# First-layer attention: inverse row sums by a trip through memory instead of TensorE transposes, with head staging moved ahead of GpSimd's products

## The chip, the cores and the metric

One core of a Trainium2 chip runs the whole program. The metric is the device time of one execution in microseconds (us). Engines: TensorE (PE, with its weight loads shown as PEld), VectorE (DVE), ScalarE (ACT), GpSimd (POOL) and SyncE (SP), which here only issues DMAs.

## What is computed

Two layers in float32 on an input of 8 x 32 x 32 x 512. The change touches the first one alone. Per image (1024 tokens, 512 channels, 8 heads of 64):

```python
x_norm = _group_norm(x, gn_scale, gn_bias).reshape(b, seq, c)
qkv = x_norm @ w_qkv + b_qkv                       # q, k, v as 8 heads of 64
weight = jnp.einsum('bhld,bhsd->bhls', q * scale, k * scale)
weight = jax.nn.softmax(weight, axis=-1)
out = jnp.einsum('bhls,bhsd->bhld', weight, v)
out = out.transpose(0, 2, 1, 3).reshape(b, seq, c)
out = out @ w_out + b_out
return (x_flat + out).reshape(b, h, w, c)
```

The second layer (a deformable attention with its own projections, a depthwise convolution and an MLP) takes the first one's output from memory, and is the same before and after.

## The kernel before

The first layer is written by hand in Bass: five instruction streams, one for each engine, with semaphores between them. Each stream loops over the 8 images; inside an image the order of the instructions is the order of the code, and there is no scheduler. Precision is kept by splitting each float32 operand of a product into a high part and a remainder (`kh`/`kl`, `ph`/`pl`, `wqkv_hi`/`wqkv_lo`), so one product is made of two or three matmuls.

**Units and pairs.** A unit u is one head and one tile of 128 queries; an image has U = 64 units, 8 a head. A pair b is two units, 32 pairs in an image, four a head. Every engine runs a loop over a step i_, and does in step i_:

- TensorE (`tensor_image`, L409): half of the products with v of pair (i_ - 5) // 2 (`output`, 8 matmuls at L484), the scores of unit i_ (`scores`, four matmuls at L448 and L449 into two PSUM banks), then the eight transposes of the exponents of unit i_ - 2 (`transposes`, L463), in two groups of four, each into one of two banks. In the odd steps, where `part == 0`, `output` also transposes the broadcast inverse row sums of the two units (L479) into the upper half of the bank in which the products of the pair are summed.
- VectorE (`vector_image`, loop at L623): the negated maximum of the scores (L626), in even steps the fold sum of a pair (L634), the two subtractions that make the low part `pl` of unit i_ - 2 (L643), and in odd steps the reciprocals of a pair's row sums (L647).
- ScalarE (`scalar_image`, loop at L563): in even steps two copies out of PSUM for a pair, `fold_t` (L570) and `fold_r` (L574), then the high part `ph` of unit i_ - 2 (L584, twice) and the exponent of unit i_ with its row sum (L591).
- GpSimd (`gpsimd_image`): for each pair the product of the fold sum with `fold_r` (L725), written over the head's q in `qk`; in between, the parts of `stage` (L704 to L716), which makes high and low parts of the next head's q and k.
- SyncE (`sync_image`): copies of each head's q and k into `qs` and `kl` (L390, L391), two tile sets in turn, then loads for the next image (L396) and of the residual (L403), and stores of the result (L406).

The high and low part of v stand side by side, so a pair's products come out as 128 partitions, of which two halves must be added: `fold_t` moves one half across, and the fold sum adds it to the other. Even heads use partitions 0 to 63 for this, odd heads 64 to 127 (`own_half`). Each 64 x 256 sum is then scaled by 1/row sum per query, and since the queries lie along the free dimension there, the inverse must stand along it too. That is what the transposes at L479 and the copy `fold_r` make.

**Waits that matter here.** The first transposes group of a unit waits for the subtraction of the same group one unit before (`pl_ok`), since there are two banks. The scores of unit i_ wait for the exponent of unit i_ - 2 and, at the first tile of a head, for the whole staging of the head (`staged`). Fold sums and `fold_r` have two buffers, so fold sum b waits for product b - 2 (`att_ok`). When four pairs of an even and four of an odd head are done, a quarter of the attention's result is split into high and low parts, in two halves behind steps 16c + 23 and 16c + 25 (`SPLIT_AT`, ScalarE L599 and VectorE L651); the last quarter is split in four pieces behind steps 64 to 70.

**The tail of an image.** Behind step 63 only the rest of the pairs is left; TensorE fills the time with transposes of the next image's tokens (`turn`, L190) and with the output projection (L510), and ScalarE copies those transposes out (`keep_tile`, L194) behind the last piece of the split.

## Time and profile before

| what | value |
| --- | --- |
| median of 3 runs (lowest to highest) | 4038.05 us (4036.7 to 4046.57) |
| the profiled execution: its time, its span | 4036.7 us, 4035.0 us |
| mean granted share of TensorE's clock | 0.987 |
| busy: TensorE, its weight loads, VectorE | 3865.6, 3260.5, 2966.9 us |
| busy: ScalarE, GpSimd | 2507.4, 1638.9 us |
| first weight load of scores, last of the L479 transposes | 92.5 us, 2294.2 us |

Busy time is the union of an engine's instructions. Matmuls are pipelined and their ends are modelled, so two neighbours overlap in the rows, and the distance between starts tells what one costs; the weight loads give these starts best. In a timeline row the first number is the start, the second the time from the first start to the last end of the merged instructions, xN their number, and the bracket the idle time before and what ended it.

### The profile page before, as it was taken

The numbers are of one execution on the slowest core, as the hardware profiler recorded it, in microseconds if no ns is written. First come the engines' busy times: TensorE is split into PE (matmuls) and PEld (weight loads), VectorE is DVE, ScalarE is ACT, GpSimd is POOL, SyncE is SP. The second block draws the span as 40 slices with busy tenths as digits, with TensorE's granted clock in tenths as the row PEclk, the third lists the DMA queues.
The fourth block names the chain that finished last, engine by engine and source line by source line (L and its number), as shares of the span: only waits on it lengthen the run. The fifth ranks groups of instructions, "written<-read, shape, count | busy, mean of one in ns | idle before, by whom it ended". The sixth has DMA issues, their size and how long they took to land. (4 is left out here: it accounts for less than half of the span.)

```text
span 4035.0 us, 63980 instructions
## 1 busy us (share of the span) xinstructions
PE 3865.6 (96%) x22126; PEld 3260.5 (81%) x22126; DVE 2966.9 (74%) x5158; ACT 2507.4 (62%) x5497; POOL 1638.9 (41%) x1935
## 2 busy tenths in 40 slices
PE   8999999999999999999999988999999999999999
PEld 6888888888888888878878856777777777777777
DVE  3984984975966957938849737878787878787876
ACT  3883864865846847838838615656565656565656
POOL 1332432422432432323324305555555555555554
PEclk9999999999999999999999989999999999999999
DMA  2221221221221221222212132222222222222221
GB/s 86 43 64 45 50 64 42 44 79 36 64 63 27 59 63 32 54 63 43 64 42 50 55 110 61 79 70 77 71 78 70 79 70 78 70 77 70 77 74 58
DMA packets 117736, 252.28 MB, mean 63 GB/s; under 512 B 17772, under 2 KB 34216, under 8 KB 117416
## 3 DMA queue, kind: packets, MB, share of 16 engines
q1 hardware_dynamic: 112808, 231.41, 21.3%
q0 software_dynamic: 4608, 16.78, 1.3%
q8 instruction: 180, 2.95, 0.3%
q14 instruction: 140, 1.15, 0.1%
HBM read 97.12 MB, written 33.55 MB: 32 GB/s over the span
## 5 line engine op out<-in xcount | busy, mean ns | idle before, releaser
L626 DVE TENSOR_REDUCE a_neg_max<-a_ps 128x1 f32<-128x1024 f32 x512 | 625.0, 1222 | 336.7 <-PE a_ps L449 336.7
L725 POOL TENSOR_TENSOR a_qk<-a_fold_s,a_fold_r 64x256 f32<-64x256 f32 x256 | 191.4, 748 | 1228.8 <-DVE a_fold_s L634 1228.8
L584 ACT ACTIVATE a_ph<-a_ps 128x512 fp32r<-128x512 f32 x1024 | 556.9, 593 | 171.3 <-PE a_ps L463 168.3
L643 DVE TENSOR_TENSOR a_pl<-a_ps,a_ph 128x512 fp32r<-128x512 f32 x1024 | 654.7, 680 | 8.9 <-ACT a_ph L584 5.7
L591 ACT ACTIVATE a_prob<-a_ps,a_neg_max 128x1024 f32<-128x1024 f32 x512 | 572.3, 1118 | 17.6 <-DVE a_neg_max L626 11.8
L463 PEld LDWEIGHTS a_ps<-a_ident,a_prob 128*128 128x128 f32 x4096 | 469.8, 140 | 112.6 <-issue 46.8
L463 PE MATMUL a_ps<-a_ident,a_prob 128*128 128x128 f32 x4096 | 540.7, 274 | 17.3 <-DVE a_pl L643 16.2
L484 PE MATMUL a_ps<-a_ph,a_v 128*128 128x256 f32 x2048 | 550.7, 302 | 0.0
L484 PE MATMUL a_ps<-a_pl,a_v 128*128 128x256 f32 x2048 | 509.2, 282 | 0.0
L448 PE MATMUL a_ps<-a_kh,a_qs 128*128 128x512 f32 x1024 | 408.3, 399 | 12.0 <-POOL a_kl L716 12.0
L449 PE MATMUL a_ps<-a_kl,a_qs 128*128 128x512 f32 x1024 | 404.8, 395 | 0.0
L1853 POOL TENSOR_SCALAR b_prob<-b_prob,b_row_inv 128x256 f32<-128x256 f32 x512 | 247.5, 483 | 365.1 <-DVE b_row_inv L1734 329.3
L484 PEld LDWEIGHTS a_ps<-a_pl,a_v 128*128 128x128 f32 x2048 | 389.3, 190 | 0.3
L484 PEld LDWEIGHTS a_ps<-a_ph,a_v 128*128 128x128 f32 x2048 | 386.5, 189 | 0.3
L1628 DVE SCALAR_TENSOR_TENSOR b_ps<-b_qpad,b_dww,b_ps 128x256 f32<-128x256 f32 x704 | 294.2, 483 | 4.8
L1550 ACT ACTIVATE b_prob<-b_ps,b_neg_max 128x256 f32<-128x256 f32 x512 | 236.5, 483 | 40.5 <-DVE b_neg_max L1739 39.9
L1298 PE MATMUL b_ps<-b_qpad,b_diag 128*128 128x256 f32 x928 | 232.4, 409 | 0.0
L448 PEld LDWEIGHTS a_ps<-a_kh,a_qs 128*128 128x128 f32 x1024 | 193.7, 189 | 43.9 <-POOL a_kl L716 21.7
L1298 PEld LDWEIGHTS b_ps<-b_qpad,b_diag 128*128 128x128 f32 x928 | 176.4, 190 | 51.0
L449 PEld LDWEIGHTS a_ps<-a_kl,a_qs 128*128 128x128 f32 x1024 | 194.1, 190 | 25.0
L250 PE MATMUL a_ps<-a_xh,wqkv_hi 128*128 128x512 f32 x512 | 200.0, 391 | 4.1 <-DVE wqkv_lo L355 4.1
L250 PE MATMUL a_ps<-a_xh,wqkv_lo 128*128 128x512 f32 x512 | 199.9, 390 | 0.0
(265 smaller groups left out, 9316.0 us busy)
## 6 DMA issues: line engine op xcount, KB each, us to landing
a_qs<-a_qk SPq DMA_DIRECT2D x128, 256.0 KB, 3.7
a_kl<-a_qk SPq DMA_DIRECT2D x128, 256.0 KB, 4.4
a_xtok<-in_x SPq DMA_DIRECT2D x64, 256.0 KB, 4.6
b_xs<-x SPq DMA_DIRECT2D x64, 256.0 KB, 4.6
b_qs<-b_qh SPq DMA_DIRECT2D x64, 256.0 KB, 3.3
b_qs<-b_ql SPq DMA_DIRECT2D x64, 256.0 KB, 3.8
b_z<-x SPq DMA_DIRECT2D x64, 256.0 KB, 3.7
out<-b_ot SPq DMA_DIRECT2D x64, 256.0 KB, 2.0
```

Source lines behind the costliest of these rows:

```text
L250: mm = pe.matmul(ps[:, g % 8, :], a, b, start=k == 0 and e == 0, stop=k == CT - 1 and e == 2)
L448: pe.matmul(bank, q_, kh[:, j, n], start=True, stop=False)
L449: mm = pe.matmul(bank, q_, kl[:, j, n], start=False, stop=True)
L463: mm = pe.transpose(ps[:, 4 + n % 2, kk * P:(kk + 1) * P], prob[:, u % 2, kt * P:(kt + 1) * P], ident[:])
L484: mm = pe.matmul(ps[:, 6 + b % 2, 0:256], v[:, h, kt, :], q_[:, b % 2, kt, :], start=kt == 0 and e == 0, stop=kt == TT - 1 and e == 1)
L584: act.activation(ph[:, b % 2, 4 * g:4 * g + 4, (u % 2) * P:(u % 2 + 1) * P], ps[:, 4 + n % 2, :].rearrange("p (k q) -> p k q", k=4), ACT.C ...
L591: act.activation(prob[:, i_ % 2, :], ps[:, 2 * (i_ % 2):2 * (i_ % 2) + 2, :] .rearrange("p a b -> p (a b)"), ACT.Exp, bias=neg_max[:, i_:i ...
L626: dve.tensor_reduce(neg_max[:, i_:i_ + 1], ps[:, 2 * (i_ % 2):2 * (i_ % 2) + 2, :] .rearrange("p a b -> p (a b)"), AX, ALU.max, negate=Tru ...
L643: dve.tensor_tensor(pl[here], ps[:, 4 + n % 2, :].rearrange("p (k q) -> p k q", k=4), raw(ph[here]), ALU.subtract).then_inc(pl_ok, 1)
L1298: mm = pe.matmul(ps[:, c, 0:NS], diag[:, e % DIAGS, :], window(c, n), start=first, stop=last)
L1628: dve.scalar_tensor_tensor(dst, window(c, n), dww[:, c, n:n + 1], grid(partial), ALU.mult, ALU.add).then_inc(tap, 1)
L1853: pool.tensor_scalar(prob[:, u % 2, t, :], prob[:, u % 2, t, :], row_inv[:, c:c + 1], 0.0, ALU.mult, ALU.add).then_inc(sc_ok, 1)
```

## The change

Inverse sums take another way. After the reciprocals of pair b, SyncE writes the 128 x 2 values of `row_inv` to a row of a small tensor in memory (`inverses_out`) and, once that write has landed, reads the row back as a broadcast over 64 partitions into `fold_r` (`inverses_in`), one pair behind. The L479 transposes and the `fold_r` copy are gone. The row in memory is ordered (query, unit of the pair), so GpSimd's product reads `fold_r` with a stride of two. `fold_r` and `fold_s` have four buffers instead of two. The reciprocals move from the odd step to the end of the even step before it. GpSimd does each part of `stage` ahead of the product beside which it stood. SyncE's stream is rearranged around the pairs: head copies, the write of pair b, the read of pair b - 1, and in the last eight pairs one load each for the next image. Waits on `fold_cp` count one copy a pair instead of two.

```diff
--- before.py
+++ after.py
@@ -84,6 +84,9 @@
     NB = TOK // 256
     U = NH * TT
     QSCALE = 1.0 / HD
+    ROWS = 4
+
+    inv_row = nc.dram_tensor("a_inv_row", [U // 2, 256], F32, kind="Internal").ap()
 
     with ExitStack() as ctx:
         def sem(name):
@@ -107,8 +110,8 @@
         row_sum = R.take("a_row_sum", [P, U])
         row_inv = R.take("a_row_inv", [P, U])
         fold_t = R.take("a_fold_t", [P, 256])
-        fold_r = R.take("a_fold_r", [P, 2, 256])
-        fold_s = R.take("a_fold_s", [P, 2, 256])
+        fold_r = R.take("a_fold_r", [P, ROWS, 256])
+        fold_s = R.take("a_fold_s", [P, ROWS, 256])
         qk = R.take("a_qk", [P, 2 * CT, TOK])
         v_at = R.at
         v = R.take("a_v", [P, NH, TT, P], F32R)
...
@@ -380,7 +386,8 @@
             at = counted(r)
             more = r + 1 < n_images
 
-            for h in range(NH):
+            def copies(h):
+
                 p, j = h // 2, h % 2
                 sp.wait_ge(qk_sb, at(qk_sb, 4 if p == 0 else 4 + 4 * p))
                 if h >= 2:
@@ -389,11 +396,36 @@
                     rows_ = slice(HD * half, HD * half + HD)
                     sp.dma_start(raw(qs[rows_, j, :]), qk[own_half(h), p, :]).then_inc(s_ld[j], 16)
                     sp.dma_start(raw(kl[rows_, j, :]), qk[own_half(h), CT + p, :]).then_inc(s_ld[j], 16)
-            if more:
-                for j in range(2):
-                    sp.wait_ge(s_ld[j], at(s_ld[j], 64 * (NH // 2)))
-                for t in range(TT):
+
+            def inverses_out(b):
+
+                sp.wait_ge(inv_ok, at(inv_ok, b + 1))
+                sp.dma_start(inv_row[b].rearrange("(p n) -> p n", n=2), row_inv[:, 2 * b:2 * b + 2])\
+                  .then_inc(iv_st[b % 2], 16)
+
+            def inverses_in(b):
+
+                sp.wait_ge(iv_st[b % 2], at(iv_st[b % 2], 16 * (b // 2 + 1)))
+                if b >= ROWS:
+                    sp.wait_ge(att_ok, at(att_ok, b - ROWS + 1))
+                sp.dma_start(fold_r[own_half(b // NB), b % ROWS, :], inv_row[b].partition_broadcast(HD))\
+                  .then_inc(iv_ld[b % ROWS], 16)
+
+            copies(0)
+            copies(1)
+            for b in range(U // 2):
+                if (b + 1) % NB == 0 and (b + 1) // NB + 1 < NH:
+                    copies((b + 1) // NB + 1)
+                inverses_out(b)
+                if b >= 1:
+                    inverses_in(b - 1)
+                if more and b >= U // 2 - TT:
+                    t = b - (U // 2 - TT)
+                    if t == 0:
+                        for j in range(2):
+                            sp.wait_ge(s_ld[j], at(s_ld[j], 64 * (NH // 2)))
                     sp.dma_start(xtok[:, t, :], x[r + 1, t * P:(t + 1) * P, :]).then_inc(x_ld[t], 16)
+            inverses_in(U // 2 - 1)
             sp.wait_ge(score, at(score, U))
             for t in range(TT):
                 if t == 2:
@@ -468,16 +500,10 @@
 
                 h = b // NB
                 if part == 0:
-                    pe.wait_ge(inv_ok, at(inv_ok, b + 1))
                     if b == 0:
                         pe.wait_ge(vl_ok, at(vl_ok, n_v))
                     if b >= 2:
                         pe.wait_ge(fold_add, at(fold_add, b - 1))
-                        pe.wait_ge(fold_cp, at(fold_cp, 2 * b - 2))
-                    for n in range(2):
-                        u = 2 * b + n
-                        pe.transpose(ps[:, 6 + b % 2, 256 + n * P:256 + (n + 1) * P],
-                                     row_inv[:, u:u + 1].to_broadcast([P, P]), ident[:])
                 pe.wait_ge(pl_ok, at(pl_ok, 4 * b + 3 + part))
                 for kt in range(4 * part, 4 * part + 4):
                     for e, q_ in enumerate((ph, pl)):
@@ -494,7 +520,6 @@
                     pe.wait_ge(pl_ok, at(pl_ok, 2 * U))
                 elif t in (2, 3):
                     pe.wait_ge(fold_add, at(fold_add, U // 2 + t - 3))
-                    pe.wait_ge(fold_cp, at(fold_cp, U + 2 * (t - 3)))
                 else:
                     pe.wait_ge(out_ok, at(out_ok, t - 3))
                 n = slice(t * P, (t + 1) * P)
@@ -568,10 +593,6 @@
                     if b >= 1:
                         act.wait_ge(fold_add, at(fold_add, b))
                     act.activation(fold_t[own_half(h), :], ps[other_half(h), 6 + b % 2, 0:256], ACT.Copy)\
-                        .then_inc(fold_cp, 1)
-                    if b >= 2:
-                        act.wait_ge(att_ok, at(att_ok, b - 1))
-                    act.activation(fold_r[own_half(h), b % 2, :], ps[own_half(h), 6 + b % 2, 256:512], ACT.Copy)\
                         .then_inc(fold_cp, 1)
                 if 2 <= i_ < U + 2:
                     u = i_ - 2
@@ -628,10 +649,10 @@
                 if 6 <= i_ <= U + 4 and i_ % 2 == 0:
                     b = (i_ - 6) // 2
                     h = b // NB
-                    dve.wait_ge(fold_cp, at(fold_cp, 2 * b + 2))
-                    if b >= 2:
-                        dve.wait_ge(att_ok, at(att_ok, b - 1))
-                    dve.tensor_tensor(fold_s[own_half(h), b % 2, :], ps[own_half(h), 6 + b % 2, 0:256],
+                    dve.wait_ge(fold_cp, at(fold_cp, b + 1))
+                    if b >= ROWS:
+                        dve.wait_ge(att_ok, at(att_ok, b - ROWS + 1))
+                    dve.tensor_tensor(fold_s[own_half(h), b % ROWS, :], ps[own_half(h), 6 + b % 2, 0:256],
                                       fold_t[own_half(h), :], ALU.add).then_inc(fold_add, 1)
                 if 2 <= i_ < U + 2:
                     u = i_ - 2
@@ -642,9 +663,9 @@
                         dve.wait_ge(ph_ok, at(ph_ok, n + 1))
                         dve.tensor_tensor(pl[here], ps[:, 4 + n % 2, :].rearrange("p (k q) -> p k q", k=4),
                                           raw(ph[here]), ALU.subtract).then_inc(pl_ok, 1)
-                    if u % 2 == 1:
-                        dve.wait_ge(exp_ok, at(exp_ok, u + 1))
-                        dve.reciprocal(row_inv[:, u - 1:u + 1], row_sum[:, u - 1:u + 1]).then_inc(inv_ok, 1)
+                if i_ >= 2 and i_ % 2 == 0 and i_ <= U:
+                    dve.wait_ge(exp_ok, at(exp_ok, i_))
+                    dve.reciprocal(row_inv[:, i_ - 2:i_], row_sum[:, i_ - 2:i_]).then_inc(inv_ok, 1)
                 if i_ in SPLIT_AT:
                     c, n = SPLIT_AT[i_]
                     dve.wait_ge(ah_ok, at(ah_ok, list(SPLIT_AT).index(i_) + 1))
@@ -720,15 +741,17 @@
             stage(1, (0, 1, 2))
             for b in range(U // 2):
                 h = b // NB
-                pool.wait_ge(fold_add, at(fold_add, b + 1))
-                pool.wait_ge(fold_cp, at(fold_cp, 2 * b + 2))
-                pool.tensor_tensor(qk[own_half(h), h // 2, (b % NB) * 256:(b % NB + 1) * 256],
-                                   fold_s[own_half(h), b % 2, :], fold_r[own_half(h), b % 2, :],
-                                   ALU.mult).then_inc(att_ok, 1)
-                pool.wait_ge(att_ok, at(att_ok, b + 1))
                 k, part = (b + 2) // NB, (b + 2) % NB
                 if 1 <= k <= NH - 2 and part < 3:
                     stage(k + 1, (part,))
+                pool.wait_ge(fold_add, at(fold_add, b + 1))
+                pool.wait_ge(iv_ld[b % ROWS], at(iv_ld[b % ROWS], 16 * (b // ROWS + 1)))
+                pool.tensor_tensor(qk[own_half(h), h // 2, (b % NB) * 256:(b % NB + 1) * 256]
+                                   .rearrange("p (n q) -> p n q", n=2),
+                                   fold_s[own_half(h), b % ROWS, :].rearrange("p (n q) -> p n q", n=2),
+                                   fold_r[own_half(h), b % ROWS, :].rearrange("p (q n) -> p n q", n=2),
+                                   ALU.mult).then_inc(att_ok, 1)
+                pool.wait_ge(att_ok, at(att_ok, b + 1))
             for t in range(TT):
                 pool.wait_ge(r_ld[t], at(r_ld[t], 16))
                 pool.tensor_tensor(tok[t], tok[t], bout[:], ALU.add).then_inc(res_ok, 1)
```

## Rows read from the trace of the kernel before

**Rows 1.** The page's busy time of each engine (us, share of the span, instructions).

```profile
PE 3865.6 (96%) x22126; PEld 3260.5 (81%) x22126; DVE 2966.9 (74%) x5158; ACT 2507.4 (62%) x5497; POOL 1638.9 (41%) x1935
```

**Rows 2.** Groups by line, L479 on TensorE: busy us, mean ns | idle before.

```profile
L479 PE MATMUL a_ps<-a_ident,a_row_inv 128*128 128x128 f32 x512 | 97.8, 273 | 0.6 <-DVE a_row_inv L647 0.6
```

**Rows 3.** Timeline of the weight loads, steps 10 to 12 (even head).

```profile
121.75 0.19 PEld L448 LDWEIGHTS a_ps<-a_kh,a_qs 128*128 128x128 f32 x1
...
123.57 0.25 PEld L479 LDWEIGHTS a_ps<-a_ident,a_row_inv 128*128 128x128 f32 x2
...
124.73 0.19 PEld L448 LDWEIGHTS a_ps<-a_kh,a_qs 128*128 128x128 f32 x1
...
127.48 0.19 PEld L448 LDWEIGHTS a_ps<-a_kh,a_qs 128*128 128x128 f32 x1
```

**Rows 4.** Timeline of VectorE behind the splits of steps 23 and 25.

```profile
164.08 0.69 DVE L651 TENSOR_TENSOR a_a<-a_qk,a_a 128x512 fp32r<-128x512 f32 x1 [0.68 <-ACT a_a L599]
164.69 1.22 DVE L626 TENSOR_REDUCE a_neg_max<-a_ps 128x1 f32<-128x1024 f32 x1
...
172.50 1.27 DVE L643 TENSOR_TENSOR a_pl<-a_ps,a_ph 128x512 fp32r<-128x512 f32 x2
```

**Rows 5.** Weight loads, first of steps 15, 16, 18, 23, 24, 28.

```profile
136.18 0.19 PEld L448 LDWEIGHTS a_ps<-a_kh,a_qs 128*128 128x128 f32 x1
...
139.53 0.19 PEld L448 LDWEIGHTS a_ps<-a_kh,a_qs 128*128 128x128 f32 x1 [0.52 <-POOL a_kl L716]
...
145.24 0.19 PEld L448 LDWEIGHTS a_ps<-a_kh,a_qs 128*128 128x128 f32 x1
...
159.67 0.19 PEld L448 LDWEIGHTS a_ps<-a_kh,a_qs 128*128 128x128 f32 x1
...
162.88 0.19 PEld L448 LDWEIGHTS a_ps<-a_kh,a_qs 128*128 128x128 f32 x1 [0.38 <-POOL a_kl L716]
...
175.16 0.19 PEld L448 LDWEIGHTS a_ps<-a_kh,a_qs 128*128 128x128 f32 x1
```

**Rows 6.** Timeline of VectorE in step 10 (even head).

```profile
123.00 1.23 DVE L626 TENSOR_REDUCE a_neg_max<-a_ps 128x1 f32<-128x1024 f32 x1 [0.26 <-PE a_ps L449]
124.14 0.41 DVE L634 TENSOR_TENSOR a_fold_s<-a_ps,a_fold_t 64x256 f32<-64x256 f32 x1
124.47 1.27 DVE L643 TENSOR_TENSOR a_pl<-a_ps,a_ph 128x512 fp32r<-128x512 f32 x2
```

**Rows 7.** Timeline of VectorE and ScalarE in step 16 (fold of an odd head).

```profile
140.76 1.23 DVE L626 TENSOR_REDUCE a_neg_max<-a_ps 128x1 f32<-128x1024 f32 x1 [0.84 <-PE a_ps L449]
141.19 1.09 ACT L584 ACTIVATE a_ph<-a_ps 128x512 fp32r<-128x512 f32 x2 [0.35 <-PE a_ps L463]
142.01 0.43 DVE L634 TENSOR_TENSOR a_fold_s<-a_ps,a_fold_t 64x256 f32<-64x256 f32 x1
142.47 1.29 DVE L643 TENSOR_TENSOR a_pl<-a_ps,a_ph 128x512 fp32r<-128x512 f32 x2
```

**Rows 8.** Timeline of GpSimd ahead of head 2's first scores.

```profile
136.28 0.74 POOL L725 TENSOR_TENSOR a_qk<-a_fold_s,a_fold_r 64x256 f32<-64x256 f32 x1 [2.87 <-DVE a_fold_s L634]
137.09 2.38 POOL L716 TENSOR_TENSOR a_kl<-a_kl,a_kh 128x1024 fp32r<-128x1024 f32 x1
```

**Rows 9.** Timeline in the tail of the second image: ScalarE, weight loads, TensorE.

```profile
569.85 0.38 ACT L574 ACTIVATE a_fold_r<-a_ps 64x256 f32<-64x256 f32 x1
...
571.69 0.95 PEld L463 LDWEIGHTS a_ps<-a_ident,a_prob 128*128 128x128 f32 x8 [0.79 <-issue]
...
584.00 2.10 PE L190 MATMUL a_ps<-a_ident,a_xtok 128*128 128x128 f32 x16 [0.80 <-ACT a_xt L194]
```

**Rows 10.** Issue of a head copy (timeline of SyncE), and landings by kind (us).

```profile
139.26 1.19 SPq L391 DMA_DIRECT2D a_kl<-a_qk  x1
...
a_kl<-a_qk SPq DMA_DIRECT2D x128, 256.0 KB, 4.4
...
b_kh<-b_kc_hi SPq DMA_DIRECT2D x128, 64.0 KB, 2.1
```

More of the change, by code:

```diff
@@ L163, in layer0 @@
         av_ps, fold_cp, fold_add, att_ok = sem("av_ps"), sem("fold_cp"), sem("fold_add"), sem("att_ok")
+        iv_st, iv_ld = [sem(f"iv_st{i}") for i in range(2)], [sem(f"iv_ld{i}") for i in range(ROWS)]
         ah_ok, al_ok, out_ps, res_ok, out_ok = sem("ah_ok"), sem("al_ok"), sem("out_ps"), sem("res_ok"), sem("out_ok")
@@ L166, in layer0 @@
                    xn_ok, xh_ok, xl_ok, pr_ps, qk_sb, vh_ok, vl_ok, staged, score, max_ok, exp_ok, tr_ps, ph_ok,
-                   pl_ok, inv_ok, av_ps, fold_cp, fold_add, att_ok, ah_ok, al_ok, out_ps, res_ok, out_ok]
+                   pl_ok, inv_ok, av_ps, fold_cp, fold_add, att_ok, *iv_st, *iv_ld, ah_ok, al_ok, out_ps, res_ok, out_ok]
         nums = [s.num for s in cleared]
@@ L368, in layer0 @@
         EACH.update({s_ld[0].num: 256, s_ld[1].num: 256, o_st.num: 16 * TT, pr_ps.num: len(groups), qk_sb.num: n_qk})
-        EACH.update({s.num: U for s in (score, max_ok, exp_ok, fold_cp)})
+        EACH.update({s.num: U for s in (score, max_ok, exp_ok)})
         EACH.update({s.num: 2 * U for s in (tr_ps, ph_ok, pl_ok)})
-        EACH.update({s.num: U // 2 for s in (inv_ok, av_ps, fold_add, att_ok)})
+        EACH.update({s.num: U // 2 for s in (inv_ok, av_ps, fold_cp, fold_add, att_ok)})
+        EACH.update({s.num: 16 * (U // 4) for s in iv_st})
+        EACH.update({s.num: 16 * (U // 2 // ROWS) for s in iv_ld})
         EACH.update({staged.num: STAGE * NH, ah_ok.num: len(SPLIT_AT), al_ok.num: len(SPLIT_AT)})
```

## Prediction

> **What bounds the kernel.** The table of busy time comes first [rows 1]: TensorE 96%, VectorE 74%, ScalarE 62%, GpSimd 41%, over both layers. The change touches the first layer's attention alone, so the second view is its costliest groups: the two transposes of inverse sums in front of each pair of units run 512 times, 0.273 us each [rows 2]. An average hides what a step costs, so the third view is the timeline of TensorE's weight loads, read from one first load of scores (L448) to the next. I call that distance a step; a step i does scores(i), the transposes of unit i-2 and half of the products with v of an earlier pair.
> In a pair of steps of an even head [rows 3] the step that holds the L479 transposes is 124.73 - 121.75 = 2.98 us long (2.97 as a rule), the other 127.48 - 124.73 = 2.75. The remaining instructions are the same, so the two transposes cost 0.22 us of TensorE's stream, not 2 x 0.273: matmuls overlap. TensorE is back to back there, hence it bounds these pairs.
> VectorE is the next bound, and nearly as close. Transposes wait for the subtractions (L643) of the unit before (two PSUM banks), and these come behind the maximum and the fold sum. The place where this loop bites is seen after a split of a finished quarter: there the subtractions end at 172.50 + 1.27 = 173.77 [rows 4] and the scores two steps on start at 175.16 [rows 5], 1.39 us later (rest of the transposes, eight products, nothing else). Below 1.39 this distance can't go. In the even head it is 127.48 - (124.47 + 1.27) = 1.74 [rows 3, 6]: 0.35 to spare. In an odd head it is 145.24 - (142.47 + 1.29) = 1.48 [rows 7, 5]: 0.09 to spare. The reason stands in the starts: in the even head the fold sum starts at 124.14, 0.09 before the maximum ends, and the subtraction at 124.47, 0.08 before the fold's end [rows 6]; in the odd one both start 0.02 to 0.03 after the end [rows 7], and maximum to last subtraction takes 3.00 us instead of 2.74.
> Why odd heads are slower decides a term. At 140.76 ScalarE is not late: it copies into ph at 141.19 after 0.35 us of idling [rows 7], and the fold still waits for the maximum's end. So the copy that the change removes (fold_r) is not what keeps VectorE apart; the partitions are, since odd heads use partitions 64 to 127. The Trainium skill, "VectorE: DVE Perf Modes", section "Two Vector instructions with no wait between them", gives the rule: an instruction whose operands start in another quadrant of 32 partitions than those before it is held until they have finished. By that rule the odd heads stay as slow as they are, since the fold keeps its partitions; without it one would book 0.22 us for their pairs too, as the first rival does. The trace agrees with the rule.
>
> **The change, part by part** (per image; 8 images).
> 1. Inverse transposes gone from TensorE. 30 of the 32 pairs have them between two steps with scores: 11 in even heads, 12 in odd ones, 6 around the splits (part 2) and one at the tail's start (part 3). Even heads: 11 pairs (step 4 and the four of head 0 make 5, and two of each of heads 2, 4, 6 outside the splits) x (2.97 - 2.75) = 2.42 us; the spare 0.35 covers it, and TensorE stays the bound. Odd heads 1, 3, 5: 12 pairs x (1.48 - 1.39) = 1.08; what is late next is the subtraction.
> 2. Heads staged ahead. The first scores of head 2 start late: 139.53 - 136.18 = 3.35 instead of 2.75, behind GpSimd's L716; head 3's 162.88 - 159.67 = 3.21 [rows 5]. L716 starts at 137.09, behind the product at 136.28, before which GpSimd idled 2.87 us [rows 8]. In the new order its 2.38 us fill that idle time and end 3 us or more before the scores. Gain 0.60 at heads 2, 4, 6. At heads 3, 5, 7 nothing: the split just before (steps 23, 39, 55) holds VectorE: its part of the split waits 0.68 us for ScalarE's and ends at 164.77, and the next maximum starts right there, at 164.69 [rows 4], when its scores are long done; from there to 175.16 all hangs on VectorE and ScalarE, which the change leaves as they are. So the 0.46 there, and the 0.22 of the two split pairs, turn into a wait for subtractions. 3 x 0.60 = 1.80.
> 3. ScalarE's fold_r copy gone: 0.38 us beside other work inside the attention, where ScalarE waits for transposes anyway: nothing. In the tail it counts. The ph copy of unit 62 follows fold_r (569.85) at once, and the last transposes (571.69, 0.79 idle) wait for that unit's subtraction [rows 9]: 0.38, and with the maximum a little earlier 0.45. Then the transposes of the last pair, 0.22. Together 0.67. The last pair's fold_r stands between its products and the x copies for which TensorE waits 0.80 us at 584.00 [rows 9]: 0.38 and the gap behind it, 0.40, in the 7 images with a next one.
> 4. Reciprocals one step earlier: 0.15 us of VectorE behind the subtractions of the even step. The exponents were done a step before, so no new wait; the maximum queued behind starts up to 0.1 later, and has the odd step (no fold) to catch up. Nothing. If that cover were gone it is 0.07 a pair, 30 pairs: 2.1 an image.
> 5. The trip through memory: 256 writes of 8 bytes a partition and 256 broadcast reads, on SyncE's queue between head copies and x loads. No row shows such a write; landings run from 2.1 us (64 KB) to 4.4 (head copies) [rows 10]. The reads' issue follows the next pair's write, whose reciprocal ends about 4.1 us into the step (the subtractions end at 125.74 - 121.75 = 3.99 [rows 3, 6], and 0.15 follows); with issues of 1.2 each, as the head copy's [rows 10], and 2.1 the row lands 4.1 + 2.4 + 2.1 = 8.6 us after that step's start, and the sum it meets is ready one pair (5.6) and 2.8 later (124.14 + 0.41 - 121.75), at 8.4. So it is 0.2 late, with 4.4 it is 2.5: GpSimd's product is late then, but nobody waits, since four sum buffers let it fall three pairs (16 us) behind. In the tail the last reciprocal is at 571.7 (an estimate: behind the subtractions for which the transposes of 571.69 waited, 0.6 for the second of them, less the 0.45 of part 3), the write lands by 575.0 (at 4.4: 577.3), the read by 578.3 (582.9), wanted at 580.9, 0.4 before the sum of today: between 2.6 us spare and 2.0 late (16 us over the images). I take spare, the 64 KB row being nearest in size. The residual loads start up to 8 us later, behind the last read; GpSimd adds the first behind the last product, at 582, and by 2.1 the first lands at 581.6: nothing, or 1 to 2 us an image if late.
> 6. Head copies queue behind one write and one read: 1.2 us later, covered by the 3 us by which staging then ends ahead of need. The x loads are spread and ready before step 64. GpSimd reads fold_r with a stride of 2: 0.74 us [rows 8], at most doubled, and hidden but for the last product (up to 0.7 x 8 = 6 us against; taken as 0).
>
> Sum: 2.42 + 1.08 + 1.80 + 0.67 = 5.97, x 8 = 47.8; 0.40 x 7 = 2.8; together 50.6 us. The profiled execution took 4036.7 us (span 4035.0); 4036.7 - 50.6 = 3986.1. The median of the three runs lies 1.35 above: 3987.5, rounded 3988.
>
> **Rivals.**
> - TensorE the bound everywhere: odd heads shed 0.22 too, 12 x 0.13 x 8 = 12 more, and with splits half relieved (3 x 0.2 x 8) 5 more: 3971. For it: fold_r is out of VectorE's wait. Against: [rows 7]. 12%.
> - VectorE the bound in even heads too (the reciprocal in the even step, ScalarE shifted): 11 x 0.13 x 8 = 11 less, and the tail's 8.2 eaten by a late row: 4007. For: 0.35 of spare shrinks to 0.13. Against: the copies get earlier, not later. 18%.
> - The trip decides: SyncE takes a pair's write and read in turn; if issue and landing block it beyond a pair (5.5 us), the product falls behind, after four pairs the fold waits for att_ok, and the excess stands in every pair: at 7 us, 256 x 1.5 = 384 us more, less the 51: 4371. It decides from 5.5 us of SyncE a pair, and turns the gain at 5.7; from rows it is 2 x 1.2 plus a quarter of four copies, 3.6 at most. The Trainium skill, "DMA: Bandwidth & Descriptors", "Specifications", speaks against the change here: below 512 B a write to memory is read, modified and written. No run here shows that yet. 5%.
> - No change: transposes and staging wait hidden anyway. Against it stands 2.98 beside 2.75 in every pair. 4%.
>
> **Chances.** Forecast 61%. Measurement tells 0.3% (12 us) from nothing. Faster: 61 + 12 + 18 = 91%; same 4%; slower 5%. Range 3968 to 4011: its lower end is the first rival, its upper the second; outside lie the last two.
>
> **What would show it.** L479 and the fold_r copy gone. Even-head pairs 5.50 us, odd ones 5.64, with TensorE waiting for the subtraction before the odd step's transposes; first step of heads 2, 4, 6 at 2.75 to 2.9; heads 3, 5, 7 a longer wait behind the split. GpSimd's product starting by the fold sum, seldom by the DMA. Wrong if odd pairs are 5.50 (first rival), if even pairs are above 5.6 (second), if the fold sum waits for a product or SyncE's queue is full (third).

## The result, and the profile after

The changed kernel takes 4025.22 us (median of 5 runs, 4022.35 to 4029.2) beside 4045.91 us of the kernel before on the same chip (5 runs): ratio 0.9954, interval 0.9943 to 0.9965. It is faster, by 0.46% or 20.7 us between the medians; forecast were 50.6 us, 1.3%. The profiled execution took 4022.35 us (span 4020.6) against 4036.7 (4035.0): 14.4 us in place of 50.6.

The page's busy times (us, share of the span, instructions), to read beside [rows 1]:

```profile
PE 3822.8 (95%) x21614; PEld 3202.9 (80%) x21614; DVE 2979.5 (74%) x5158; ACT 2433.8 (61%) x5241; POOL 1641.5 (41%) x1935
```

TensorE has lost 512 transposes and ScalarE 256 copies, as the code says. VectorE has as many instructions as before and is busy 12.6 us longer. That is the first sign.

Every local term of the forecast is there. Weight loads, first of steps 10 to 12, of the changed kernel (compare [rows 3]):

```profile
124.24 0.19 PEld L480 LDWEIGHTS a_ps<-a_kh,a_qs 128*128 128x128 f32 x1
...
126.99 0.19 PEld L480 LDWEIGHTS a_ps<-a_kh,a_qs 128*128 128x128 f32 x1
...
129.74 0.19 PEld L480 LDWEIGHTS a_ps<-a_kh,a_qs 128*128 128x128 f32 x1
```

A pair of an even head takes 2.75 + 2.75 = 5.50 us (5.72 before). An odd head, first the weight loads (first of steps 15, 16 and 18), then VectorE (compare [rows 5, 7]):

```profile
138.00 0.19 PEld L480 LDWEIGHTS a_ps<-a_kh,a_qs 128*128 128x128 f32 x1
...
140.88 0.19 PEld L480 LDWEIGHTS a_ps<-a_kh,a_qs 128*128 128x128 f32 x1
...
144.65 0.95 PEld L495 LDWEIGHTS a_ps<-a_ident,a_prob 128*128 128x128 f32 x8 [0.24 <-issue]
...
146.51 0.19 PEld L480 LDWEIGHTS a_ps<-a_kh,a_qs 128*128 128x128 f32 x1
```

```profile
142.13 1.23 DVE L647 TENSOR_REDUCE a_neg_max<-a_ps 128x1 f32<-128x1024 f32 x1 [0.24 <-PE a_ps L481]
143.38 0.43 DVE L655 TENSOR_TENSOR a_fold_s<-a_ps,a_fold_t 64x256 f32<-64x256 f32 x1
143.84 1.29 DVE L664 TENSOR_TENSOR a_pl<-a_ps,a_ph 128x512 fp32r<-128x512 f32 x2
```

The pair takes 5.63 us (forecast 5.64), the fold sum starts 1.25 behind the maximum's start, and TensorE idles 0.24 us before the odd step's transposes. Step 15, behind which head 2's first scores come, takes 140.88 - 138.00 = 2.88 us (3.35 before; forecast 2.75 to 2.9). With step 14 it takes 5.63 us in place of 6.32: 0.69 less, the 0.60 booked for head 2 and the 0.09 booked for an odd pair.

The loss shows when the starts of scores are summed over whole images (us, from one profile of each kernel; the last column is the changed kernel with one wait added, e11 below):

| stretch | before | changed | with the wait |
| --- | --- | --- | --- |
| up to the first scores | 92.5 | 95.6 | 92.8 |
| steps 0 to 62, eight images | 1469.4 | 1459.6 | 1427.5 |
| from step 62 to the next image's first scores, seven | 720.4 | 712.9 | 709.5 |
| last step 62 to the second layer | 39.9 | 38.6 | 38.6 |
| second layer | 1712.7 | 1713.9 | 1711.8 |
| span | 4035.0 | 4020.6 | 3980.3 |

The first and the fifth row hold work that the change leaves alone, and they vary by some us from profile to profile; the rows between them are 18.6 us shorter in the changed kernel than before. With the wait, steps 0 to 62 take 178.44 us in every image, 5.24 less than the 183.68 before (forecast 5.30). The changed kernel's images take 179.4 to 185.3 instead. The excess sits in steps 22 to 28 and 38 to 46, behind the splits of the first and second quarter. One of these places, in image 2 (timeline of all engines):

```profile
498.55 1.06 POOL L725 TENSOR_SCALAR a_kh<-a_qs 128x1024 fp32r<-128x1024 f32 x1 [1.93 <-DMA a_kl<-a_qk]
...
499.69 2.40 POOL L727 TENSOR_TENSOR a_qs<-a_qs,a_kh 64x1024 fp32r<-64x1024 f32 x1
...
499.94 2.69 DVE L672 TENSOR_TENSOR a_a<-a_qk,a_a 128x512 fp32r<-128x512 f32 x1 [0.61 <-ACT a_a L620]
...
502.56 1.21 DVE L647 TENSOR_REDUCE a_neg_max<-a_ps 128x1 f32<-128x1024 f32 x1
...
504.81 0.96 PEld L495 LDWEIGHTS a_ps<-a_ident,a_prob 128*128 128x128 f32 x8 [2.95 <-issue]
```

The split's subtraction (L672), 0.69 us in [rows 4], lasts 2.69. It began 0.25 us behind GpSimd's L727, which belongs to the staging of head 6, and ends 0.54 us behind L727's end (502.09). Maximum and transposes queue behind it. The new order starts staging as soon as the head's copies have landed ([1.93 <-DMA]), not behind a product; for heads 4 and 6 that falls on the split. The same instruction in all images, by source line: minimum/median/maximum ns, before and then changed:

```profile
L651 DVE TENSOR_TENSOR a_a<-a_qk,a_a x48: 691/693/694, 164.1 to 2271.9; 128x512 fp32r<-128x512 f32 x48
```

```profile
L672 DVE TENSOR_TENSOR a_a<-a_qk,a_a x48: 691/693/2692, 164.9 to 2257.8; 128x512 fp32r<-128x512 f32 x48
```

14 of the 48 are held, 21.3 us together beyond 0.69 each: ten by L727, and four by L725, the instruction before it in the staging (0.85 to 1.47 us). Steps 0 to 62 lost 1459.6 - 1427.5 = 32.1 us. The other 10.8 are put down to TensorE's clock. Windows around the same place (us busy and count for PE, PEld, DVE, ACT, POOL; granted clock; DMA share; GB/s):

```profile
500.00:504.00 4.00, 2.29 (x16) 1.77 (x14) 4.00 (x3) 1.60 (x4) 2.09 (x1) 1.00 0.00 0
504.00:508.00 4.00, 3.16 (x18) 2.98 (x19) 3.68 (x7) 3.48 (x7) 2.83 (x3) 0.76 0.07 17
508.00:512.00 4.00, 4.00 (x23) 3.40 (x23) 2.70 (x5) 2.24 (x5) 0.94 (x2) 0.82 0.00 0
```

TensorE was busy 2.29 of 4.00 us during the hold; then the granted clock is 0.76 and 0.82, a stretch at the lower level (1.2 GHz) worth (0.24 + 0.18) x 4 = 1.7 us. Seven such stretches lie in steps 0 to 62 of the changed kernel, each beginning 2 to 4 us behind the end of one of the ten longest holds (1.8 to 2.0 us each), and none in the kernel with the wait. Seven times 1.7 is 11.9, near the 10.8 left over. Three of the ten have no such stretch behind them; why, the runs don't tell.

### The profile page after: what moved, and what is told of

It is laid out like the page before. It is cut to its first block and busy times, and to the rows that moved or that the text cites. A ratio compares the mean times of both kernels' runs of the same rounds, so it can differ in the third digit from the quotient of the medians.

```text
span 4020.6 us, 63404 instructions
## 1 busy us (share of the span) xinstructions
PE 3822.8 (95%) x21614; PEld 3202.9 (80%) x21614; DVE 2979.5 (74%) x5158; ACT 2433.8 (61%) x5241; POOL 1641.5 (41%) x1935
## 3 DMA queue, kind: packets, MB, share of 16 engines
q0 software_dynamic: 4608, 16.78, 1.4%
q8 instruction: 176, 2.88, 0.3%
## 5 line engine op out<-in xcount | busy, mean ns | idle before, releaser
L605 ACT ACTIVATE a_ph<-a_ps 128x512 fp32r<-128x512 f32 x1024 | 565.8, 598 | 198.2 <-PE a_ps L495 196.8
L495 PE MATMUL a_ps<-a_ident,a_prob 128*128 128x128 f32 x4096 | 557.7, 278 | 56.7 <-DVE a_pl L664 55.6
L725 POOL TENSOR_SCALAR a_kh<-a_qs 128x1024 fp32r<-128x1024 f32 x64 | 67.9, 1061 | 359.2 <-DMA a_kl<-a_qk 358.5
```

Of the source, the lines that this page charges most:

```text
L495: mm = pe.transpose(ps[:, 4 + n % 2, kk * P:(kk + 1) * P], prob[:, u % 2, kt * P:(kt + 1) * P], ident[:])
L605: act.activation(ph[:, b % 2, 4 * g:4 * g + 4, (u % 2) * P:(u % 2 + 1) * P], ps[:, 4 + n % 2, :].rearrange("p (k q) -> p k q", k=4), ACT.C ...
```

## The experiments

Theory: GpSimd's staging holds VectorE's split subtraction. Rivals: the staging order or the split in itself, or the trip through memory, costs the time. Times of different groups are compared by their ratios to the kernel before. The kernels of one group ran on one chip, beside the kernel before: 4039.42 us for the first four, 4045.84 for the next four, 4035.8 for the last four.

**e1: the changed kernel, staging behind the product again.**

```diff
-                k, part = (b + 2) // NB, (b + 2) % NB
-                if 1 <= k <= NH - 2 and part < 3:
-                    stage(k + 1, (part,))
...
                 pool.wait_ge(att_ok, at(att_ok, b + 1))
+                k, part = (b + 2) // NB, (b + 2) % NB
+                if 1 <= k <= NH - 2 and part < 3:
+                    stage(k + 1, (part,))
```

> The changed kernel with one part undone: GpSimd does each part of the head staging behind the product again. Collision theory (a VectorE instruction with two operands in SBUF waits until a GpSimd instruction that has begun is done, and the changed order lays GpSimd's 2.40 us subtraction for heads 4 and 6 beside VectorE's 0.69 us subtraction of the splits at steps 25 and 41): none of the six split subtractions of an image is above 0.72 us; steps 22 to 28 take 18.3 to 18.5 us and not up to 21.5; the staging wait is back at heads 2, 4, 6 (steps 14 to 16 take about 6.3 us). Against the kernel before about 34 us less, so faster than the changed kernel by about 14. Rival (the late trip of the inverse rows and of the head copies on SyncE's queue costs the time, whatever GpSimd does when): the trip is unchanged, so steps 22 to 28 stay at up to 21.5 us, and with the staging waits back it is 10 us slower than the changed kernel.

4010.83 us (5 runs), ratio 0.9927 (0.9913 to 0.994), 0.3% or some 12 us below that of the changed kernel: undoing one part of the change is a gain. None of the 48 split subtractions of the attention lasts above 0.70 us. Head 2's first scores are late again, 3.59 us behind step 15's start in place of 2.88. Weight loads, then GpSimd:

```profile
136.99 0.19 PEld L480 LDWEIGHTS a_ps<-a_kh,a_qs 128*128 128x128 f32 x1
...
140.58 0.19 PEld L480 LDWEIGHTS a_ps<-a_kh,a_qs 128*128 128x128 f32 x1 [0.63 <-POOL a_kl L737]
```

```profile
137.31 0.76 POOL L746 TENSOR_TENSOR a_qk<-a_fold_s,a_fold_r 64x256 f32<-64x256 f32 x1 [2.65 <-DVE a_fold_s L655]
138.14 2.38 POOL L737 TENSOR_TENSOR a_kl<-a_kl,a_kh 128x1024 fp32r<-128x1024 f32 x1
```

So staging ahead is worth its place at heads 2, 4 and 6, and costs more than that at the splits: steps 0 to 62 take 1449.2 us, less than the changed kernel's 1459.6 and more than the 1427.5 with the wait.

**e2: the kernel before, with staging ahead alone** (the reverse move).

> The kernel before with one part of the change alone: staging ahead of the products; inverse sums still through TensorE's transposes. Collision theory: waits of 0.60 us at heads 2, 4, 6 go (14 us less), those of 0.46 at heads 3, 5, 7 turn into waits for the split; but VectorE's split subtraction at step 25 or 41 now waits for GpSimd in several images, up to 2 us each, 10 to 30 us in all: between 10 us less and 15 us more than before. Rival (the trip on SyncE's queue is the cost): there is no trip here, so 14 us less than before and no split subtraction above 0.72 us.

4044.39 us (11 runs), ratio 1.001 (1.0001 to 1.0019): no gain alone. All 16 splits at these two places (steps 25 and 41) are held, 16.8 us in all. Steps 0 to 62 take 1477.0 us against 1469.4: the 14.4 booked for heads 2, 4 and 6 are outweighed by the holds and by three stretches at the lower clock. (This profile is of the slowest of the 11 runs, 4059.16 us.) One of them, VectorE and then GpSimd:

```profile
457.69 2.23 DVE L651 TENSOR_TENSOR a_a<-a_qk,a_a 128x512 fp32r<-128x512 f32 x1 [0.60 <-ACT a_a L599]
```

```profile
456.99 2.38 POOL L706 TENSOR_TENSOR a_qs<-a_qs,a_kh 64x1024 fp32r<-64x1024 f32 x1
```

The hold needs neither the trip nor the four buffers.

**e3 and e11: the changed kernel, GpSimd's first part of heads 4 and 6 waits for the split.**

```diff
                 if 0 in parts:
+                    if h in (4, 6):
+                        pool.wait_ge(al_ok, at(al_ok, h - 2))
```

> The changed kernel with one wait added: GpSimd begins the staging of heads 4 and 6 only when VectorE's second split subtraction (steps 25 and 41) is done. Collision theory: no split subtraction above 0.72 us, every image's steps 0 to 62 at 178.5 us (now 179.4 to 185.3), 32 us less than the changed kernel's profile of 4022.4, so about 3990, and 1.2% under the kernel before. Rival (late rows and copies): rows and copies come as before and GpSimd does its work later still, so no gain, or a loss of up to 10 us.

3989.43 us (4 runs), ratio 0.9877 (0.9862 to 0.9892). Run again beside the changed kernel itself:

> The kernel that makes GpSimd wait for the split, again, beside the others on one chip: no held subtraction, steps 0 to 62 at 1427.5 us for eight images, and 0.988 of the kernel before, 0.7% below the changed kernel (about 28 to 36 us). If its gain was the chip's, it would come out at the changed kernel's time.

> The changed kernel itself once more, to stand beside the three others on one chip. It should come out at 0.995 of the kernel before, with 10 to 16 split subtractions of VectorE held by GpSimd.

3984.49 (ratio 0.9878, 0.9858 to 0.9897) against 4023.65 for the changed kernel (e10, 7 runs, ratio 0.9961, 0.9948 to 0.9974; 15 held subtractions, 22.3 us): 39 us between the medians, from one wait that makes GpSimd later. In the two profiles 32.7 us of it lie in steps 0 to 62 and 1.7 in the tails; the second layer, which the wait doesn't touch, differs by 10 us between them, so the last few us can't be placed. The group of the split subtractions in e10, then in e11 (busy us, mean ns | idle before):

```profile
L672 DVE TENSOR_TENSOR a_a<-a_qk,a_a 128x512 fp32r<-128x512 f32 x48 | 54.6, 1137 | 32.6 <-ACT a_a L620 32.6
```

```profile
L672 DVE TENSOR_TENSOR a_a<-a_qk,a_a 128x512 fp32r<-128x512 f32 x48 | 33.2, 693 | 32.4 <-ACT a_a L620 32.4
```

With the wait the forecast's sum comes out: 50.6 us against 50.0 and 51.3 measured in the two groups. The trip is as it was in the changed kernel, so it is no rival for the loss, and the theory stands.

**e4: the changed kernel, L727 with one operand in place of two** (q's low part is left out).

```diff
-                    pool.tensor_tensor(qs[HD:P, j, :], raw(qs[HD:P, j, :]), raw(hi[HD:P, :]), ALU.subtract)\
+                    pool.tensor_scalar(qs[HD:P, j, :], raw(qs[HD:P, j, :]), 0.0, 0.0, ALU.mult, ALU.add)\
```

> The changed kernel with GpSimd's low part of q (64 x 1024, two operands in SBUF, 2.40 us) made by an instruction with one operand; it writes zeros, so the low part of q is left out of the scores. Theory that any GpSimd instruction holds VectorE's two-operand subtraction until it ends: the instruction takes about 1.05 us, split subtractions still reach 1.2 to 1.7 us where they meet it, steps 22 to 28 at most 19.5 us, 15 to 25 us less than the changed kernel. Theory that only GpSimd instructions with two operands hold it: all split subtractions at 0.69 us, steps 22 to 28 at 18.25 us, 32 us less.

3999.08 us (4 runs), ratio 0.9902 (0.9887 to 0.9917). VectorE, then GpSimd:

```profile
450.49 1.35 DVE L672 TENSOR_TENSOR a_a<-a_qk,a_a 128x512 fp32r<-128x512 f32 x1 [0.60 <-ACT a_a L620]
```

```profile
450.26 1.04 POOL L727 TENSOR_SCALAR a_qs<-a_qs 64x1024 fp32r<-64x1024 f32 x1
```

A GpSimd instruction with one operand holds VectorE as well, as L725 did in the changed kernel: the subtraction ends at 451.84, again 0.54 behind GpSimd's end. What counts is how long the instruction lasts. The holds in the attention sum to 8.1 us instead of 21.3, and three quarters of the loss in steps 0 to 62 is gone (1435.8). No stretch at the lower clock lies in these steps, though 15 subtractions are held; none of these holds adds more than 0.9 us.

**e5 and e12: e3, with the folded sums of every head in partitions 0 to 63** (`fold_t`, `fold_s`, `fold_r`).

```diff
-                    act.activation(fold_t[own_half(h), :], ps[other_half(h), 6 + b % 2, 0:256], ACT.Copy)\
+                    act.activation(fold_t[0:HD, :], ps[HD:P, 6 + b % 2, 0:256], ACT.Copy)\
...
-                    dve.tensor_tensor(fold_s[own_half(h), b % ROWS, :], ps[own_half(h), 6 + b % 2, 0:256],
-                                      fold_t[own_half(h), :], ALU.add).then_inc(fold_add, 1)
+                    dve.tensor_tensor(fold_s[0:HD, b % ROWS, :], ps[0:HD, 6 + b % 2, 0:256],
+                                      fold_t[0:HD, :], ALU.add).then_inc(fold_add, 1)
...
-                sp.dma_start(fold_r[own_half(b // NB), b % ROWS, :], inv_row[b].partition_broadcast(HD))\
+                sp.dma_start(fold_r[0:HD, b % ROWS, :], inv_row[b].partition_broadcast(HD))\
...
```

GpSimd's product reads `fold_s` and `fold_r` there and still writes the head's own half of `qk`.

> The changed kernel with the wait of the run before, and with the fold of every head made in partitions 0 to 63 (fold_t, fold_s and fold_r there; GpSimd's product writes the head's own half). Theory that VectorE's fold sum and its neighbours are kept apart in odd heads by the partitions: all pairs outside the splits take 5.50 us, the fold sum starts 1.14 us behind the maximum's start everywhere (not 1.26), steps 14 to 22 take 22.0 us (now 22.53): 12 pairs x 0.13 x 8 images = 12 us less than 3989, so 3977. Rival (odd heads are slower because of the data's place in PSUM or of ScalarE's part): nothing changes, 3989.

3988.71 us (5 runs), ratio 0.9856 (0.9833 to 0.9879). And beside e11 on one chip:

> The kernel with the folded sums in the lower partitions for every head, on the same chip as the one it is built on. Steps 0 to 62 give 12.0 us (0.125 us for each of 96 pairs of odd heads). The theory that the clock gives it back: the tail of each image has one stretch at the lower clock, 1.4 to 1.7 us longer, in seven or eight images instead of one, and the two kernels differ by 0 to 5 us. The rival, that those stretches fall by chance on either kernel: 8 to 14 us below it.

3983.92 us (4 runs), ratio 0.9868 (0.9849 to 0.9888). VectorE in an odd head of e12:

```profile
138.72 1.22 DVE L647 TENSOR_REDUCE a_neg_max<-a_ps 128x1 f32<-128x1024 f32 x1 [0.33 <-PE a_ps L481]
139.86 0.41 DVE L655 TENSOR_TENSOR a_fold_s<-a_ps,a_fold_t 64x256 f32<-64x256 f32 x1
```

The fold sum starts 1.14 behind the maximum's start, not 1.25, and overlaps its end. Odd pairs take 5.50 us, and steps 0 to 62 take 12.0 us less (1415.5). So it is the partitions of the fold that held odd heads at 5.63: the prediction's reason is shown. (The edit moves the half of PSUM that the sum reads together with its operand in SBUF; which of the two counts, it doesn't tell.) Yet the time hardly moves: 0.6 us in the last group. The tails take back 8.5 (718.0 against 709.5): six of seven take 102.8 us, against 101.4 in e11. Windows in the tail of image 2, e12 and then e11:

```profile
577.40:587.40 10.00, 7.82 (x33) 6.08 (x32) 9.08 (x9) 2.72 (x3) 6.27 (x5) 0.97 0.12 44
587.40:597.40 10.00, 10.00 (x40) 8.12 (x39) 5.88 (x8) 1.52 (x2) 0.00 (x0) 0.86 0.30 111
```

```profile
581.00:591.00 10.00, 7.80 (x35) 6.15 (x34) 8.84 (x9) 2.50 (x3) 6.49 (x5) 1.00 0.12 44
591.00:601.00 10.00, 10.00 (x46) 8.27 (x45) 6.11 (x8) 1.74 (x2) 0.00 (x0) 1.00 0.32 120
```

Both were busy 7.8 of 10 us before; only e12's granted clock then falls, to 0.86. Why there and not in e11, the runs don't tell. That the clock gives back most of the gain is what these rows show: six stretches of 1.4 to 1.7 us. The remaining 3 us are less than the 6.4 by which the second layer differs between the two profiles.

**e6: e3, with VectorE's part of the split one step later.**

```diff
-                if i_ in SPLIT_AT:
-                    c, n = SPLIT_AT[i_]
+                at_ = i_ if i_ >= U else i_ - 1
+                if at_ in SPLIT_AT and (at_ < U - 1 or i_ >= U):
+                    c, n = SPLIT_AT[at_]
...
```

> The changed kernel with the wait on the split subtraction, and with VectorE's six split subtractions of an image done one step later, at the end of steps 24, 26 and so on, so that VectorE does not wait 0.6 us for ScalarE's half of the split in front of the next maximum. If the wait for ScalarE, and not VectorE's 0.69 us of work, is most of what a split costs: steps 22 to 30 take 22.5 us instead of 23.74, 1.2 x 3 x 8 = 29 us less than 3989, so 3960 (at least 3975). Rival (the work itself is the cost, the wait only fills what TensorE leaves): 3985 to 3990.

3965.11 us (5 runs, 3955.09 to 3973.47), ratio 0.9803 (0.9779 to 0.9827). VectorE in steps 24 and 25:

```profile
164.92 0.15 DVE L668 RECIPROCAL a_row_inv<-a_row_sum 128x2 f32<-128x2 f32 x1
164.99 0.66 DVE L673 TENSOR_TENSOR a_a<-a_qk,a_a 128x512 fp32r<-128x512 f32 x1
165.58 1.21 DVE L647 TENSOR_REDUCE a_neg_max<-a_ps 128x1 f32<-128x1024 f32 x1
```

The idle time before the subtraction (0.68 us in [rows 4]) is gone. Steps 22 to 28 take 16.78 us instead of 18.23, steps 0 to 62 28.1 less over eight images. Three of the moved subtractions meet GpSimd again, 0.9 us in all. This wait was in the kernel before too.

**e7: e3, reading pair b - 1's row before writing pair b's.**

```diff
-                inverses_out(b)
                 if b >= 1:
                     inverses_in(b - 1)
+                inverses_out(b)
```

> The changed kernel with the wait on the split subtraction, and with the row of pair b-1 read back before pair b is written, so that it lands some 3 us sooner. Theory that the trip is hidden behind four buffers: GpSimd waits less for rows (now 220 us in all), and the time stays at 3989 within 3 us. Rival (late rows still cost time, in the tail or at the splits): at least 5 us less.

3999.05 us (6 runs), ratio 0.9883 (0.9861 to 0.9904), that of e3. GpSimd's waits for the row, in e11, e7 and e9 (us in total, times, longest):

```profile
POOL a_qk L751 <- DMA a_fold_r<-a_inv_row: 189.8, 53, 5.8
```

```profile
POOL a_qk L751 <- DMA a_fold_r<-a_inv_row: 96.2, 21, 7.5
```

```profile
POOL a_qk L751 <- DMA a_fold_r<-a_inv_row: 984.2, 183, 47.2
```

Half of the wait is gone and no scores move: 178.5 us an image. The last product of an image starts up to 4.5 us behind the end of its sum (at most 0.3 in e3), and the tails grow to 722.5 us, about half of it by four stretches at the lower clock. So the row's lateness costs nothing in the attention; why the last row comes later in this order was not followed up.

**e8: e5 and e6 together.**

> The two edits of the low half and of the late split together. If both theories hold the gains add up, 12 and 29 us: 3948. If VectorE's work is the bound behind the splits, less: up to 3977.

3961.68 us (5 runs), ratio 0.9785 (0.9761 to 0.9809). Steps 0 to 62 take 1386.8 us, 12.6 under e6: there the two gains add up. But the tails take 716.3 against 709.5, with five stretches at the lower clock, and the second layer, which no edit touches, 12.5 more in this profile; the medians of e6 and e8 are not told apart. Both beat the two kernels of the case by 1.5% and more.

**e9: e3, with the reciprocals back at the odd step.**

```diff
-                if i_ >= 2 and i_ % 2 == 0 and i_ <= U:
-                    dve.wait_ge(exp_ok, at(exp_ok, i_))
-                    dve.reciprocal(row_inv[:, i_ - 2:i_], row_sum[:, i_ - 2:i_]).then_inc(inv_ok, 1)
+                if i_ >= 3 and i_ % 2 == 1 and i_ <= U + 1:
+                    dve.wait_ge(exp_ok, at(exp_ok, i_ - 1))
+                    dve.reciprocal(row_inv[:, i_ - 3:i_ - 1], row_sum[:, i_ - 3:i_ - 1]).then_inc(inv_ok, 1)
```

> The kernel that makes GpSimd wait for the split (3989), with the reciprocals back at the odd step. The theory that the trip lies in slack inside attention: the row of inverses comes one step, about 2.75 us, later at each pair; the product waits for it up to 5.0 us instead of 2.3 us behind the folded sum, and GpSimd's staging and residuals move with it, but the scores keep their starts: steps 0 to 62 of an image stay at 178.4 us (1427.5 us for eight), and only the last product of an image, on which the next stage waits, costs 1 to 2.7 us: 7 to 20 us in all, 3997 to 4010 us. The rival, that the trip decides (the third of the prediction): every pair pays the 2.75 us less what is hidden, and steps 0 to 62 grow by over 10 us an image: over 4070 us.

3993.88 us (4 runs), ratio 0.9894 (0.9878 to 0.991): 9.4 us above e11. The row is now what the product waits for in 183 of 256 pairs (the third row above), 984 us in total, of which 368 are GpSimd's idle time ahead of the eight images' first products, and steps 0 to 62 stay at 1427.2. The tails pay 11.0 us, 6 of them in four stretches at the lower clock (101.4 to 101.6 us where neither intervenes, up to 104.9). The trip lies in slack inside the attention, and on the path at an image's end.

## Why the prediction was wrong

The sign and nearly all terms were right, the time was not: 4025.22 lies 14 us above the range. Part of this is the starting point, since the kernel before came out 7.9 us higher in its five runs than in the three that the prediction had; but the gain of 20.7 us also stays below the 27 of the range's upper end.

- *Inverse transposes (part 1).* Right: 5.50 and 5.63 us a pair. That odd heads are held by their partitions was argued from [rows 7] and is shown by e5. The first rival (5.50 everywhere) is false for this kernel.
- *Heads staged ahead (part 2).* The step that failed. It said "In the new order its 2.38 us fill that idle time", and of the splits that "from there to 175.16 all hangs on VectorE and ScalarE, which the change leaves as they are". The first holds for the scores of heads 2, 4 and 6, which are no longer late (0.7 us each as a rule against e1). The second is false. GpSimd's idle time was not free: what runs in it holds VectorE, if VectorE then reads both operands from SBUF. At steps 25 and 41 staging falls on the split, and VectorE's 0.69 us become up to 2.69: 21.3 us of holds and 10.8 more, put down to the lower clock behind them, of the 42 that steps 0 to 62 would have given. The prediction's sum has no term for it. e1, e2, e3 and e4 each move the holds and the time of these steps together.
- *What could have been read.* The trace of before has the hold once in each tail, where the last part of the split meets GpSimd's residual. VectorE and GpSimd of the kernel before:

```profile
581.77 0.43 DVE L651 TENSOR_TENSOR a_al_last<-a_qk,a_a 128x256 fp32r<-128x256 f32 x1
583.27 1.15 DVE L651 TENSOR_TENSOR a_al_last<-a_qk,a_a 128x256 fp32r<-128x256 f32 x1 [1.08 <-ACT a_a L599]
```

```profile
582.87 3.94 POOL L734 TENSOR_TENSOR a_tok_a<-a_tok_a,a_bout 128x512 f32<-128x512 f32 x3
```

The first of GpSimd's three instructions merged here ends at 584.14, and the held subtraction 0.28 behind it. One form, one size, 0.43 and 1.15 us: a mean hides it, the maximum of a source line shows it. The Trainium skill states the rule too, "SBUF — State Buffer", section "Who interferes with whom": a VectorE instruction with two SBUF inputs contends with a GpSimd instruction that reads SBUF, and the one that comes second is blocked until the first has finished. The trace agrees with that rule in every held row here, and in the other direction too: in the five places where the split subtraction runs ahead of L727, L727 lasts 2.68 to 2.80 us instead of 2.39. The prediction, which weighed two other rules, should have weighed this one: each GpSimd instruction that is moved, against each two-operand instruction of VectorE.
- *Tails (part 3).* 1.3 us an image against 1.07, the last one 1.3 against 0.67. The two idle times of [rows 9], 0.79 and 0.80 us, are 0.46 and 0.27 in the changed kernel. With the 0.22 of the transposes that makes 1.08; what gives the rest, and why the last image gains as much without x copies, stays open. Weight loads and TensorE:

```profile
568.56 0.95 PEld L495 LDWEIGHTS a_ps<-a_ident,a_prob 128*128 128x128 f32 x8 [0.46 <-issue]
```

```profile
580.12 2.09 PE L194 MATMUL a_ps<-a_ident,a_xtok 128*128 128x128 f32 x16 [0.27 <-ACT a_xt L198]
```

- *Reciprocals (part 4).* Nothing in the attention, right; without the move the late row costs 9.4 us (e9).
- *The trip (part 5).* Its sizes were off, its price was not. Issues of SyncE, and landings (median us):

```profile
497.05 0.33 SPq L403 DMA_DIRECT2D a_inv_row<-a_row_inv  x1
497.47 0.46 SPq L411 DMA_DIRECT2D a_fold_r<-a_inv_row  x1
```

```profile
a_fold_r<-a_inv_row SPq DMA_DIRECT2D x256, 64.0 KB, 3.6
...
x<-a_tok_a SPq DMA_DIRECT2D x48, 256.0 KB, 2.0
...
a_inv_row<-a_row_inv SPq DMA_DIRECT2D x256, 1.0 KB, 3.3
```

Issues are cheaper than the 1.2 taken, landings in the median later than the 2.1 taken, within the bound of 4.4. The product waits for the row in 59 of 256 pairs, not seldom, and the scores don't wait for the product. The third rival falls.
- *Chances.* None of the rivals named contention. The range stood on the terms' own errors, and these were right to 0.3 us an image.

## What to carry to other kernels

Before work is moved into an engine's idle time, look at what the neighbour engine runs there: here a stretch in which GpSimd was idle was free only while VectorE didn't read two operands from SBUF. A wait that makes the less loaded engine later can be the gain (39 us here from one wait). And take local gains to the end of the loop before they are booked: a step table by image showed at once that 5.24 us an image were there and half of them lost again.

## What the hardware showed unexpectedly

- The hold is exclusive, not a sharing: VectorE's 128x512 subtraction ends 0.54 us behind GpSimd's end, whether GpSimd's instruction takes 2.40 us (two operands) or 1.04 (one), and the 128x256 one 0.28 behind it. VectorE's maxima and `pl` subtractions, with one operand or none in SBUF, ran beside L727 and L737 of the changed kernel at 1.2 and 0.68 us, as fast as elsewhere.
- A hold of 2.0 us cost 3.6 in steps 38 to 46 of image 2 (27.30 against 23.73): the lower clock behind it accounts for the rest (1.7 by the windows above).
- A write of 1 KB to memory, 8 bytes a partition, lands in 3.3 us, later than a store of 256 KB (2.0). The Trainium skill, "DMA: Bandwidth & Descriptors", section "Specifications", says that below 512 B the DMA engine reads, modifies and writes. No run here separates that from other causes: the broadcast read of the row, which writes 1 KB to each partition, lands as late (3.6).
